# Attention maxima by blocks of 32 queries of four heads, turned by the vector engine, with shorter score matmuls on the diagonal

## The reference

```python
q, k = rope(split_heads(x @ Wq.T + bq)), rope(split_heads(x @ Wk.T + bk))   # (2, 16, 2048, 16)
v = split_heads(x @ Wv.T + bv)
att = jnp.einsum('bhqd,bhkd->bhqk', q, k) / 4.0
att = jax.nn.softmax(jnp.where(tril, att, -jnp.inf), axis=-1)
y = jnp.einsum('bhqk,bhkd->bhqd', att, v)
x = x + y.transpose(0, 2, 1, 3).reshape(2, 2048, 256) @ Wo.T + bo           # x was normalised before
h = silu(fp4_linear(ln(x), w_gate)) * fp4_linear(ln(x), w_up)               # 256 -> 704
x = x + fp4_linear(h, w_down)                                               # 704 -> 256
```

## Time and profile before

| | |
|---|---|
| median of three runs | 1334.23 us (1332.19 to 1339.9) |
| the profiled execution | 1329.79 us, of which the span is 1327.6 us |
| PE busy | 1266.5 us, 95% |
| DVE busy | 1088.6 us, 82% |
| ACT busy | 792.5 us, 60% |
| POOL busy | 472.1 us, 36% |
| chain that ended last | PE 76%, DVE 15%, ACT 3%, POOL 3% |
| first-pass matmuls L860 and masks L866 | 5120 and 2048 |
| second-pass matmuls L883 and masks L887 | 5120 and 2048 |
| maxima L1282 | 1120 instructions, 690.3 us |
| exponentials L1182 | 1280 instructions, 605.2 us |

### The profile page before, as it was taken

How to read it: one execution, slowest core, us unless ns; L and a number is a source line. 1 busy time by engine, 2 the same in 40 slices (tenths; PEclk the granted TensorE clock), 3 DMA queues, 4 the chain that set the end, 5 groups by cost and what they waited for, 6 DMA issues and landing times.

```text
span 1327.6 us, 43992 instructions
## 1 busy us (share of the span) xinstructions
PE 1266.5 (95%) x19062; PEld 821.1 (62%) x19062; DVE 1088.6 (82%) x2242; ACT 792.5 (60%) x1691; POOL 472.1 (36%) x499
## 2 busy tenths in 40 slices
PE   7679999999999999999999999999999999999967
PEld 6456555555666775666576766566765676855445
DVE  5788898989899897986468979889998898984256
ACT  5346667666567665675655647555665585766621
POOL 2944664653112203113355651313122312023346
PEclk9879999999999999999999999999999999999989
DMA  4634132202110110101023222111100100000000
GB/s 107 171 93 114 51 86 70 80 19 58 34 34 2 42 27 18 27 3 43 13 66 90 62 67 57 34 34 34 26 18 26 42 2 14 7 1 18 13 13 16
DMA packets 56988, 57.54 MB, mean 43 GB/s; under 512 B 10062, under 2 KB 50384, under 8 KB 56784
## 3 DMA queue, kind: packets, MB, share of 16 engines
q1 hardware_dynamic: 55496, 53.66, 15.0%
q10 hardware_dynamic: 1300, 1.08, 0.3%
HBM read 37.55 MB, written 16.78 MB: 41 GB/s over the span
## 4 chain that ended last, share of the span: by engine, by line
PE 76%; DVE 15%; ACT 3%; POOL 3%; issue 2%; DMA 1%; SPq 0%; ACTq 0%; POOLq 0%; DVEq 0%
PE bank L906 16%; PE bank L860 15%; PE bank L883 14%; PE bank L918 13%; DVE piece_max L1282 7%; PE bank L1038 5%; PE bank L978 4%; ACT prob L1182 2%; PE bank L986 2%; PE bank L1029 1%; PE bank L913 1%; PE bank L887 1%; PE bank L866 1%; DVE c_mem L1354 1%; DVE c_mem L1344 1%
## 5 line engine op out<-in xcount | busy, mean ns | idle before, releaser
L1182 ACT ACTIVATE prob<-bank 128x512 f32<-128x512 f32 (+3 forms) x1280 | 605.2, 539 | 280.5 <-PE bank L883 160.2
L1282 DVE TENSOR_REDUCE piece_max<-bank 128x1 f32<-128x512 f32 (+3 forms) x1120 | 690.3, 662 | 26.3 <-PE bank L860 11.9
L860 PE MATMUL bank<-k_mem,q_mem 96*32 96x512 bf16 (+3 forms) x5120 | 441.2, 351 | 7.3 <-DVE piece_max L1282 4.8
L883 PE MATMUL bank<-q_mem,k_mem 99*32 99x512 bf16 (+3 forms) x5120 | 443.6, 349 | 4.3 <-DVE piece_max L1282 2.4
L906 PE MATMUL bank<-prob,V 128*32 128x512 f32 (+3 forms) x2560 | 309.2, 531 | 6.6 <-ACT prob L1182 6.0
L883 PEld LDWEIGHTS bank<-q_mem,k_mem 99*32 99x32 bf16 x5120 | 190.2, 96 | 124.0 <-issue 63.1
L860 PEld LDWEIGHTS bank<-k_mem,q_mem 96*32 96x32 bf16 x5120 | 188.5, 97 | 116.3 <-issue 63.5
L1490 POOL TENSOR_TENSOR c_mem<-c_mem 128x256 f32<-128x256 f32 (+2 forms) x74 | 85.5, 1156 | 474.9 <-DVE c_mem L1366 474.9
L887 PE MATMUL bank<-mask_kq,ident_h 128*32 128x128 bf16 (+3 forms) x2048 | 129.8, 200 | 0.0
L866 PE MATMUL bank<-mask_qk,ident_h 128*32 128x32 bf16 (+3 forms) x2048 | 116.6, 203 | 0.0
L906 PEld LDWEIGHTS bank<-prob,V 128*32 128x32 f32 x2560 | 84.4, 110 | 42.0 <-ACT prob L1182 17.6
(11 more groups left out here) (174 smaller groups left out, 1412.8 us busy)
## 6 DMA issues: line engine op xcount, KB each, us to landing
parts_dram<-a_mem SPq DMA_DIRECT2D x13, 512.0 KB, 3.3
q_mem<-parts_dram SPq DMA_DIRECT2D x32, 192.0 KB, 2.9
k_mem<-parts_dram SPq DMA_DIRECT2D x32, 192.0 KB, 3.5
q_mem<-parts_dram SPq DMA_DIRECT2D x32, 128.0 KB, 3.1
k_mem<-parts_dram SPq DMA_DIRECT2D x32, 128.0 KB, 3.4
c_mem<-in_L_attn_x SPq DMA_DIRECT2D x30, 128.0 KB, 2.1
out<-c_mem SPq DMA_DIRECT2D x30, 128.0 KB, 1.7
a_mem<-in_L_attn_x SPq DMA_DIRECT2D x13, 256.0 KB, 2.6
```

The lines of the kernel that those rows point to most:

```text
L860: m = pe.matmul(b[q0:q0 + COLUMNS, j * keys:(j + 1) * keys], q_rows(u)[0:TERM_ROWS, h, i * P + q0:i * P + q0 + COLUMNS], k_rows(k0 // CHUN ...
L883: mm = pe.matmul(b[k0:k0 + COLUMNS, off:CHUNK], k_rows(j // TPC, g)[:, h, first:first + COLUMNS], q_rows(u)[:, h, off:CHUNK], start=True, ...
L1182: act.activation(prob[:, n % NP, off:CHUNK], bank_of("st", n)[:, off:CHUNK], ACT.Exp, scale=SCALE).then_inc(drained("st", n)[0], 1)
L1282: dve.tensor_reduce(piece_max[:, u % 2, h0:h0 + len(heads), slot], src.rearrange("p (h k) -> p h k", k=keys), AX.X, ALU.max).then_inc(drai ...
```

## The change

The first pass takes its scores by blocks of 32 queries of all four heads: the four divided matmuls that run side by side now have the same 32 queries of four heads, each with its own head's keys. On the diagonal block n (0 to 15) of a unit has (n+1) x 32 keys instead of a multiple of 128, and one mask of 32 columns for each head. Blocks n and 14-n share a bank (480 and 32 keys, 448 and 64, and so on), which VectorE reduces with two instructions; blocks 7 and 15 have a bank each. The whole chunks come first and no longer wait for the unit's own keys. The maxima are now laid out as (head, query of 32) x block, so that one VectorE transpose in squares of 32 makes the rows; TensorE's transposes, their bank and ScalarE's copy are gone, and the three DMAs read 64 runs of 32 elements each instead of 4 runs of 512. In the second pass, the four matmuls of a diagonal step leave out the queries that lie before their 32 keys (0, 32, 64 and 96 columns fewer); the masks stay. GpSimd sets a zero column in the parts once. The planner's costs follow.

```diff
-        for i in range(TPC):
-            width = (c * TPC + i + 1) * P
-            rest = width % BANK
-            pieces += [(u, i, [h], j * BANK, BANK, j, (j + 1) * BANK == width)
-                       for h in range(GROUP) for j in range(width // BANK)]
...
+        pieces += [(u, [(0, n, j * BANK, BANK, j, False)]) for n in range(BLOCKS) for j in range(c)]
+        for n in range(BLOCKS // 2):
+            of = [n, BLOCKS - 2 - n] if 2 * n < BLOCKS - 2 else [n]
+            widths = [(n_ + 1) * COLUMNS for n_ in of]
+            pieces.append((u, [(sum(widths[:m]), n_, c * BANK, widths[m], c, True) for m, n_ in enumerate(of)]))
+        pieces.append((u, [(0, BLOCKS - 1, c * BANK, BANK, c, True)]))
...
# planner
-            yield from plan.through(("s1", n), 0.428 * len(heads) * keys + 59 * len(heads) * masked,
-                                    "dve", 66 + 1.04 * len(heads) * keys, [("masks",)], [], divided=True)
+            yield from plan.through(("s1", n), 0.428 * keys + 29 * len(parts) * own,
+                                    "dve", 66 * len(parts) + 1.04 * keys, [("masks",)], [], divided=True)
...
-                yield from plan.through(("st", n), 0.43 * (CHUNK - off) + 59 * (j >= c * TPC), "act",
+                yield from plan.through(("st", n), 0.43 * (CHUNK - off) + 20 * (j >= c * TPC), "act",
...
# place_maxima: the three DMAs
-                engine.dma_start(q_rows(u)[TERM_ROWS + p:TERM_ROWS + p + 1, :, :],
-                                 max_rows[p * GROUP:(p + 1) * GROUP, u % 2, :]).then_inc(max_placed[u % 2], 16)
+                engine.dma_start(q_rows(u)[TERM_ROWS + p:TERM_ROWS + p + 1].rearrange("o h t -> o (h t)"),
+                                 max_rows[p % 2:P:2, u % 2, p // 2, :]).then_inc(max_placed[u % 2], 16)
...
# TensorE, first pass
+                    for column, block, k0, keys, _, own in parts:
+                        of = slice(column, column + keys)
...
+                        for h in range(GROUP):
+                            m = pe.matmul(b[COLUMNS * h:COLUMNS * (h + 1), of],
+                                          q_rows(u)[0:TERM_ROWS, h, block * COLUMNS:(block + 1) * COLUMNS],
                                           k_rows(k0 // CHUNK, g)[0:TERM_ROWS, h, k0 % CHUNK:k0 % CHUNK + keys],
-                                          start=True, stop=not masked)
+                                          start=True, stop=not own)
+                        for h in range(GROUP if own else 0):
+                            m = pe.matmul(b[COLUMNS * h:COLUMNS * (h + 1), of.stop - COLUMNS:of.stop],
+                                          ident_h[:, 0:COLUMNS], mask_qk[:, 0:COLUMNS], start=False, stop=True)
...
# TensorE, second pass
-                            first = (j % TPC) * P + k0
-                            mm = pe.matmul(b[k0:k0 + COLUMNS, off:CHUNK], k_rows(j // TPC, g)[:, h, first:first + COLUMNS],
-                                           q_rows(u)[:, h, off:CHUNK], start=True, stop=not masked)
+                            first, since = (j % TPC) * P + k0, off + k0 * masked
+                            mm = pe.matmul(b[k0:k0 + COLUMNS, since:CHUNK], k_rows(j // TPC, g)[:, h, first:first + COLUMNS],
+                                           q_rows(u)[:, h, since:CHUNK], start=True, stop=not masked, skip_group_check=masked)
...
# ScalarE
-            def drain_maxima(u):
-                yield when["drain", "maxT", u]
...
# VectorE
+                    for column, block, _, keys, slot, _ in parts:
+                        r = dve.tensor_reduce(piece_max[:, u % 2, block, slot:slot + 1],
+                                              bank_of("s1", n)[:, column:column + keys], AX.X, ALU.max)
...
+                dve.transpose(max_rows[:, u % 2].rearrange("p b t -> p (b t)"),
+                              max_parts[:, u % 2].rearrange("p b n o -> p (b n o)")).then_inc(done, 1)
```

More of the change, by code:

```diff
@@ L357, in rehearse_maxima @@
     def rehearse_maxima():
-        for n, (u, i, heads, k0, keys, slot, masked) in enumerate(pieces):
-            yield from plan.wait([("deal q", u, len(RUNS) - 1), ("deal k", u, len(RUNS) - 1)] + ([("place", u - 2, 2)] if u >= 2 else [])
+        for n, (u, parts) in enumerate(pieces):
+            keys, own = sum(part[3] for part in parts), parts[0][5]
+            yield from plan.wait([("deal q", u, len(RUNS) - 1)] + ([("deal k", u, len(RUNS) - 1)] if own else [])
+                                 + ([("place", u - 2, 2)] if u >= 2 else [])
                                  + ([("drain", "s1", n - S_IN_FLIGHT)] if n >= S_IN_FLIGHT else []))
-            yield from plan.through(("s1", n), 0.428 * len(heads) * keys + 59 * len(heads) * masked,
-                                    "dve", 66 + 1.04 * len(heads) * keys, [("masks",)], [], divided=True)
+            yield from plan.through(("s1", n), 0.428 * keys + 29 * len(parts) * own,
+                                    "dve", 66 * len(parts) + 1.04 * keys, [("masks",)], [], divided=True)
             if n == final_piece[u]:
@@ L1070, in tensor_engine @@
                     *(feed_forward(t) for t in range(len(tiles))),
-                    fill(turn_bias, "bias"), *(fill(turn_maxima, "maxT", u) for u in range(len(units))),
+                    fill(turn_bias, "bias"),
                     *(fill(turn_output, "oT", u) for u in range(len(units))))
@@ L1233, in scalar_engine @@
                     *(project_features(z, o, name) for z in range(len(pairs)) for o, name in enumerate(("q", "k"))),
-                    *(drain_maxima(u) for u in range(len(units))),
                     *(place_maxima(act, at, u) for u in range(len(units)) if placed_by_scalar(u)),
@@ L1274, in maxima @@
             def maxima():
-                for n, (u, i, heads, k0, keys, slot, _) in enumerate(pieces):
+                for n, (u, parts) in enumerate(pieces):
                     yield when["drain", "s1", n]
@@ new lines, in place_maxima @@
+                at.wait_ge(done, first + 2)
+                dve.tensor_tensor(rest, whole, high, ALU.subtract).then_inc(done, 1)
+                yield when["neg3", u]
+                at.wait_ge(done, first + 3)
+                dve.tensor_copy(middle, rest).then_inc(done, 1)
+                yield when["neg4", u]
+                at.wait_ge(done, first + 4)
+                dve.tensor_tensor(low, rest, middle, ALU.subtract).then_inc(done, 1)
+                yield when["neg5", u]
+                at.wait_ge(done, first + 5)
```

91 lines of the change are left out of this document (29 added, 62 removed).

## The result

The changed kernel took 1328.18 us (median of 9; 1325.32 to 1331.39) against 1335.37 us before (median of 9; 1332.19 to 1339.9). The ratio is 0.9948, 95% interval 0.9931 to 0.9965. It is faster by 7 us, where 34 were forecast, and outside the range. The profiled execution took 1327.12 us, span 1324.8 us. The profiled execution of the kernel before lay 5.6 us under its median, this one 1.1 us, so the two spans differ by less than the medians do.

What follows compares the result with a forecast made beforehand. TensorE was taken to bound: its 38 us saved, counted at 78%, give 30 us, VectorE 1, the start 1. 32 us off 1329.8 is 1298, or 1302 off the median; forecast 1300 us, 8-in-10 range 1281 to 1326.

Steps and rivals of the forecast that it cites:

- Which engine bounds: Whole kernel: TensorE is the bound with 76% of the chain, VectorE close behind with 15%.
- The first pass on the diagonal: First-pass diagonal scores on TensorE: fewer columns and narrower masks save 0.53 us a unit, 17 us (10 to 27).
- The rival of a floor for narrow sets: First-pass diagonal: four 32-column matmuls take 0.10 us instead of 0.03, leaving no change, 1328 to 1334 us; chance 0.07.
- The rival of slower streams: First-pass score sets: four heads' keys side by side stream slower than one head's; at 25% slower 1343 us; chance 0.06.
- The second pass on the diagonal: Second-pass diagonal on TensorE: leaving out masked queries saves 25 ns a head, half at 128 columns; 11 us (0 to 16).
- The turned maxima: TensorE's transposes of the maxima: removing them saves 0.35 us for each of 32, 11 us (7 to 13).
- VectorE: VectorE: diagonal reduces fall by 14 us, new transposes at 0.2 us add 6; net 8 us less work.
- The rival that VectorE takes over: VectorE: narrow reduces cost 151 ns before their columns and transposes 0.39 us, 40 us more work; 1317 us; chance 0.14.
- ScalarE, DMAs, the start: 32 ScalarE copies of 0.58 us removed: nothing, save 1 us gained in the first units; DMAs left at nothing.
- The sum: Whole kernel: TensorE's 38 us at 78% of the chain give 30, VectorE 1, the start 1: 32 us less.
- The fourth rival: Planner's order: a spare bank and sooner pieces give a better order, 10 us more gained, 1288 us; chance 0.07.

Runs made afterwards that it cites:

- its fastest version: The changed kernel with four planner priorities altered (st 100, w -700, place 3000, tile 300), operations unchanged: 1296.8 us, ratio 0.9706.
- the one good order: The changed kernel with `place=3000`, its second pass taking the masked queries on the diagonal again: 1321.0 us, ratio 0.989, against 1310.3 us without them.
- `place=3000`: The changed kernel with the small steps that place the maxima preferred by 3000 ns instead of 1000 in the planner: 1310.3 us, ratio 0.9818.
- the poor one: The changed kernel with one planner priority altered (projections wait 1000 ns longer, a -1000): 1358.3 us, ratio 1.0176.
- the fill: The changed kernel with 3, 1 and 5 throwaway matmuls where TensorE waits for GpSimd's rounded weights: 1328.5 us, ratio 0.995.

## Why the prediction was wrong

**Which engine bounds.** Right. TensorE has 71% of the chain in the changed kernel and in its fastest version; VectorE has 16% and 17%.

**The first pass on the diagonal.** Right in size. Masks at 0.03 us a set are what was taken. PE's busy time fell by 31 us in all, for all of the edits together. The rival of a floor for narrow sets falls: 32-column mains start 0.04 us before their masks even with the clock low (80.24 and 80.28 us in the timeline above), and masks pass in 0.03. The floor of 25 ns per matmul for 1 to 64 columns, which the Trainium skill states (TensorE: Matmul & The Clock Gate, section Back-to-back issue gap), is not paid four times by divided matmuls here: a set of four passes in about that time. The rival of slower streams falls as well: whole-chunk sets start 0.22 us apart as before, and PE would have had to be busy longer, not 31 us less.

**The second pass on the diagonal.** Right in sign, and too large in its working: a head of 128 columns takes 0.02 us less, not the half of 25 ns, but the wider ones 12 to 14 ns rather than 25. That makes 7 us of TensorE's time in all, where 11 were taken. In the one good order where it was tried it is worth 10.7 us, in the old one 1.8, so neither 11 us nor any one number was its price.

**The turned maxima.** The size fits: 11 us of TensorE's time were forecast, and doing the transposes once more costs some 10 us in the old order. That run adds them and doesn't remove them, and has no setting of the array in it.

**VectorE.** Right. The reduces fell by 14.7 us (14 forecast), a narrow one keeps to one line with the wide (182 ns for 32 elements, 646 for 480: 1.04 ns an element) and the next starts 98 ns behind it, 65 ns more than its columns, where the rival had 151. The transpose takes 235 ns where 200 were taken, and the sum is 9.4 us less, 8 forecast. The rival that VectorE takes over falls with it.

**ScalarE, DMAs, the start.** ScalarE has 19.4 us less to do; no run tests what that is worth by itself. The start was wrong: 1 us was to be gained, and the first unit's output copy came 9.4 us later: 5 us since a weight's turning blocked PE's queue, the rest on ScalarE's queue behind DMAs that waited for VectorE. The prediction looked at ScalarE's order up to the first exponentials, but not at what PE's queue holds between the first unit's maxima and its second pass. The DMAs, left at nothing, make PE wait 1.0 us between 66 and 1260 us in this order, but 8.6 with `place=3000` and 11.6 in the poor one.

**The sum.** This is the step that failed. It took TensorE's 38 us times TensorE's share of the chain, 78%, as if the rest of the time stood still. That share says how much of the time went through TensorE in the old order. The change altered the planner's costs, so each engine got a new order, and PE's idle time grew by 28 us in the profiled executions, which is all but 3 of the 31 us that its busy time fell. (The profiled execution before was a fast one; against the 66.2 us of the run with the transposes done twice, in the same order, the growth is 23.) The fourth rival had a new order in it, but only as a gain; that the new order could be worse had no chance of its own. With the priorities altered alike in both kernels, the operations are worth 22 and 37 us; with each kernel's best set 24; with the priorities as they are 7. The forecast of 34 lies in that spread, but only one of these pairs reaches it. The planner itself had less to give: its ends for the two kernels, 1309.8 and 1286.1 us, differ by 24 us, which could have been read before any run. The range was too narrow by what order alone does: the old operations spanned 27 us in four orders, the new ones 61 in five.

**What stays open.** The early loss can be read in the trace, as two weights in a row on PE's queue and the placing DMAs on ScalarE's; no run moved either by itself. For the later ones (400 to 800 us) the runs show that order removes most of them, not which instruction's place is at fault. The measured time lies 24 to 28 us above the planned end for the four old orders in the table and 37 to 56 for the new ones; so of the 24 us that the planner saw, 17 were lost to something that it doesn't reckon with, and every new order loses some of this. The clock may be part of it. PE was busy for 45 of the changed kernel's 71 us at the lower level, and for 20 of the 37 before; by an estimate from these, the lower clock took up to half of the 25 us more, some 12 us. It doesn't explain the difference between the changed kernel and `place=3000`, and the fill didn't test it where PE works. Why the old order hides the second pass's saving was not tried either.

## What to carry to other kernels

Where a planner makes the order, a change of its costs is two changes: price the operations from the rows, and treat the new order as a draw whose spread is measured with the operations fixed, by running old and new under several of the planner's settings. Before that, look at both orders at the first places where the bounding engine waits: what stands on its queue ahead of the work that everything waits for. Compare the planner's own ends too: within each of the two kernels a later planned end went with a longer time, except where two planned ends lay within 5 us of each other. After such a change retune the planner's priorities, since settings that suited the old costs can hide most of a gain: with four other priorities the changed kernel takes 1296.8 us instead of 1328.2. Of those 31 us, the old operations get 14 by a set of their own.

## What the runs showed of the hardware

Sets of four divided matmuls with 32 columns pass in about 0.03 us, a set of 512 columns in 0.22, whether the four read one head's keys or four heads'. VectorE's maximum over n elements of a bank takes about 148 + 1.04 n ns, and the next starts 65 + 1.04 n ns behind it (98 ns at 32 elements, 598 at 512). Its transpose of 128 x 64 bf16 in squares of 32 takes 235 ns in the mean. Raising the granted clock from 0.50 to 0.77 over 27 us in which PE mainly waited changed the time by nothing that can be measured; it was at 0.50 again when the work went on.
